# A routed expert layer with a state-space layer: when the first tiles are masked, where the threshold search runs, and how the one-hots lie

## The chip, the cores and the metric

One Trainium2 chip, one of its cores. The metric is the device time of one execution of the kernel in microseconds (us); a lower one is better.

## The reference, cut to what matters

The input is 16 batches of 512 tokens with 256 channels. Each token is normalised; the result goes through a state-space layer (64 states) and through a layer of 8 experts, of which each token uses one.

```python
xn = layernorm(x)
# state-space layer
Bu = einsum('bld,nd->bln', xn, B_w)
h  = causal convolution of Bu with lam ** t          # a first-order recurrence
y  = einsum('bln,dn->bld', h, C_w) + D * xn
# experts
aff   = (xn @ waff.T) / (|xn| * |waff| + 1e-9)       # [16, 512, 8]
cap   = clip(floor(512 * sigmoid(aff.mean() - threshold)), 4, 512)
tcr   = one_hot(argmax(softmax(aff)), 8)
ecr   = rank of the token within its batch and expert < cap
mask  = tcr * ecr
for e in range(8):                                   # masked tokens, exact gelu
    acc += gelu((xn * mask[e]) @ W1[e] + b1[e]) @ W2[e] + b2[e]
out = x + y + acc
```

A token that is not kept by its expert still gets each expert's answer to a zero row, `gelu(b1[e]) @ W2[e] + b2[e]`, so does every token for the experts it does not use.

## The kernel before, in words

The kernel has one function, `moe_ssm_kernel`, with a program for each engine; the programs wait for each other by semaphores, and the order of work on each engine is written out by hand. Line numbers are those of the profile.

**Batches (0 to about 150 us).** A loop over 16 batches normalises, turns, runs the recurrence (VectorE, `tensor_tensor_scan`, L899) and the state products (TensorE, `states_out`, L662). GpSimd adds `D * xn + x` (L381, L385); VectorE adds the state result (`add_y`, L905). Normalised rows and base rows are stored to DRAM. Beside it the expert weights are loaded and split into a high and a low f16 part (ScalarE L513, VectorE `low_part` L928); 12 of 16 weights are ready before the tiles start, four second-layer weights (12 to 15, `LATE`) come later through one buffer, `raw_late`, loaded by SP (L336 to L340).

**Routing.** From the affinities VectorE takes the expert of each token (L1036 to L1046). Two things are then worked out beside each other:

- *The capacity threshold.* VectorE computes the capacity and turns the affinity rows into integer keys (L1052 to L1072). ScalarE finds the key of the last kept token bit by bit: `find` (L563) makes 14 digits on the upper halves, each of three dependent instructions (L565 to L567); VectorE then forms the second keys (`second_digits`, L1127), and `find` makes 16 more digits. `second_half` (L574) is called between digits: after digit 8 it copies the zero rows of the experts out of PSUM (L520), after digit 10 it splits the rows of tile 0 (L586).
- *The slots.* TensorE counts the tokens of each expert (L709, L710). VectorE gives each token a place, a high digit among 78 half tiles and a low digit among 128 rows, and makes one-hots of both in four groups of 16 token columns (`places`, L1110): L1119 and L1124 over 16 x 78 elements, L1123 over 16 x 128. In a group the token column is the outer dimension; the place value is read with stride 0 inside. TensorE multiplies them (`tokens_of`, L729) between the zero rows of the experts (`zero_row`, L713). VectorE turns the product into the token indices of all slots (L1154 to L1161).

**Tiles.** There are 39 tiles of 256 slots (`NT`), each of one expert. GpSimd gathers a tile's normalised rows (`step`, L409: L420), later its base rows (L444), and scatters the result (L434). TensorE turns the rows (`rows_t`, L771), ScalarE and VectorE split them in two f16 parts (L586, L1233), TensorE makes the first product (`up`, L781, 96 matmuls), ScalarE the gelu (L596), VectorE the two parts of h (`h_parts`, L1237), TensorE the second product (`down`, L798, 96 matmuls), and VectorE the result (`result`, L1250: L1255 takes it from PSUM, L1261 applies the mask and adds the base row, L1268 adds the zero rows' sum). On TensorE a step is: rows of tile j+1, up j, down j-1. The first 8 steps (`PEEL`) are written out, the others are a loop of two steps.

**The first two steps** carry what is left of routing. In step 0 VectorE waits for the search's result and makes the kept flags (`kept`, L1167), then the h parts of tile 0. TensorE turns the flags (`kept_rows`, L748), VectorE multiplies the one-hot planes by them (`kept_places`, L1189) and scales the late weights (`late_scales`, L920). In step 1 TensorE multiplies again (`kept_slots`, L761, 64 matmuls), VectorE makes `mask_slot` (`kept_mask`, L1202), and down 0 follows. Only then does SP load the late weights.

Of the kernel before, what the change touches and what calls it, by code (L numbers as in the profile page):

```python
# [11 lines left out]
P = 128  # L12


def moe_ssm_kernel(nc, u, log_lambda, B_w, C_w, D_w, waff, W1, b1, W2, b2, threshold, out, xn_dram, base_dram, num_dram):
# [24 lines left out]
    PEEL = 8  # L40
# [10 lines left out]
    with ExitStack() as ctx:  # L51
# [16 lines left out]
        slot_val = sb("slot_val", B)  # L68
# [60 lines left out]
        lo16 = part(area, (UNITS - 4) * UW, T * P // 2).bitcast(F16).rearrange("p (t l) -> p t l", l=P)  # L129
# [6 lines left out]
        dxn = part(work, 3 * QD, QD)  # L136
        g_bc = part(work, 4 * QD, E * D)
# [5 lines left out]
        planes = [x.bitcast(F16).rearrange("p (t j) -> p t j", j=NS) for x in planes]  # L143
        den = key_hi
# [3 lines left out]
        xnorm, sq0, ratio = pos, hi_f, lo_f  # L148
        hi16, low16 = hi_f.bitcast(F16)[:, 0:T], lo_f.bitcast(F16)[:, 0:T]
# [42 lines left out]
        def psum(name, cols):  # L192
# [7 lines left out]
        ps_bu = [ps_bu0, ps_bu1]  # L200

# [14 lines left out]
            "dve_chain", "r_pool", "bmax_ok", "bmax_out", "bmax_in", "bmax_used", "scales_ok",  # L216
# [6 lines left out]
        def zero_out(i):  # L223

            return [ps_g[:, 0:2 * D], ps_t[:, S:S + 2 * D], ps_y[:, 0:2 * D], ps_y[:, 2 * D:4 * D]][i]
# [36 lines left out]
        def _(sp):  # L262
# [73 lines left out]
            sp.wait_ge(s["mask_ok"], 1)  # L336
# [7 lines left out]
        def _(pool):  # L344
# [16 lines left out]
            link(g.iota(iota_i[:, 0:B], [[S, 4], [1, Q]], base=1, channel_multiplier=Q))  # L361
            link(g.tensor_copy(slot_val[:, :], iota_i[:, 0:B]))
# [46 lines left out]
            def step(m, r, gate_no):  # L409

                t_out, t_base = m - 5, m - 3
                if is_tile(m):
                    wait(pool, s["f_xt"], m - 1)
                    gate(gate_no)
                    g.tensor_copy(idx_x[:, 2 * r:2 * r + 2], idx_all[:, bass.ds(m * 2, 2)]).then_inc(s["ix"], 1)
                    pool.wait_ge(s["ix"], m + 1)
                    gate(gate_no + 1)
                    gate_no = gate_no + 2
                    for h in range(2):
                        g.indirect_dma_start(out=xg[r % 2][:, h * D:(h + 1) * D], out_offset=None, in_=xn_dram,  # L420
                                             in_offset=bass.IndirectOffsetOnAxis(
                                                 ap=idx_x[:, 2 * r + h:2 * r + h + 1], axis=0),
                                             bounds_check=bound, oob_is_err=False).then_inc(gx[r % 2], 16)
                rb = (r + 1) % 4
# [6 lines left out]
                if is_tile(t_out):  # L431
                    ro = (r + 3) % 4
# [15 lines left out]
                return gate_no  # L448
            gates = 0
            for m in range(8):  # L450
                if m == 3:

                    for n in range(8):
                        pool.wait_ge(base_out[n], 16)
                    for p in range(2):
                        g.memset(bg[p], 0.0).then_inc(s["cleared"], 1)
                    pool.wait_ge(s["cleared"], 4)
                gates = step(m, m % 4, gates)
                if m == 2:
                    for e in range(E):  # L460
                        add_zero_row(e)
# [11 lines left out]
        def _(act):  # L473
# [73 lines left out]

            act.wait_ge(s["aff_ok"], 1)
# [782 lines left out]
```

## Time and profile before

| | us |
|---|---|
| median of 3 runs | 661.86 (659.16 to 662.46) |
| the profiled execution | 663.84 |
| its span in the profile | 662.1 |

| engine | busy us | share of the span | instructions |
|---|---|---|---|
| PE (TensorE matmul) | 589.7 | 89% | 4597 |
| PEld (weight load) | 497.0 | 75% | 4598 |
| DVE (VectorE) | 512.2 | 77% | 974 |
| ACT (ScalarE) | 337.3 | 51% | 635 |
| POOL (GpSimd) | 462.6 | 70% | 625 |

The span in 40 slices of 16.6 us, busy tenths:

```profile
PE   2988888858945599999999999999999999999994
DVE  5789989799998979987667768676767676767672
ACT  5776868825799235644433435353535353535340
POOL 1999997920038838888776768787777787788453
PEclk9988868776997799999999999999999999999998
```

A digit is the busy share in tenths, in PEclk the clock that the throttle granted TensorE. Slices 9 to 14 (149 to 248 us) hold routing and the first steps, the others to the right are tile steps alone. A busy PE is not PE at its peak: its ends are modelled. The chain of waits follows the work back from the last instruction; a timeline lists instructions in order of time.

### The profile page before, as it was taken

The page shows a single profiled execution, that of the slowest core. Times are in us where ns is not written, and L with a number is a line of the kernel's source. Part 1 is how long each engine was busy: PE and PEld are TensorE (multiplying, and loading weights), DVE is VectorE, ACT ScalarE, POOL GpSimd, SP SyncE. Part 2 cuts the span into 40 slices and gives each one's busy share as a digit, 9 for nine tenths or more (in the row PEclk, how much of TensorE's full clock was granted, in tenths as well). Part 3 has the DMA queues.
Part 4 walks back from the last instruction along what each step waited for, and adds up shares of the span by engine and source line. Part 5 has one row for each costly group of instructions (what it writes and reads, how often), then busy time and mean ns, then how long its engine had stood idle before and what let it go on. Part 6 is the DMA issues. An engine that isn't in the chain of part 4 may idle for free.

```text
span 662.1 us, 16027 instructions
## 1 busy us (share of the span) xinstructions
PE 589.7 (89%) x4597; PEld 497.0 (75%) x4598; DVE 512.2 (77%) x974; ACT 337.3 (51%) x635; POOL 462.6 (70%) x625
## 2 busy tenths in 40 slices
PE   2988888858945599999999999999999999999994
PEld 1655555546834499898988888989898989898983
DVE  5789989799998979987667768676767676767672
ACT  5776868825799235644433435353535353535340
POOL 1999997920038838888776768787777787788453
PEclk9988868776997799999999999999999999999998
DMA  8985757611801134512212112212112212210100
GB/s 308 413 346 173 253 208 266 230 75 43 274 18 33 40 97 153 169 57 74 72 57 70 54 53 66 75 50 79 49 44 71 67 48 67 63 60 24 51 29 2
DMA packets 33584, 72.58 MB, mean 110 GB/s; under 512 B 6519, under 2 KB 19088, under 8 KB 33552
## 3 DMA queue, kind: packets, MB, share of 16 engines
q1 hardware_dynamic: 21488, 46.67, 19.7%
q0 software_dynamic: 11232, 25.20, 12.4%
q10 hardware_dynamic: 832, 0.31, 0.2%
q8 instruction: 17, 0.28, 0.2%
q14 instruction: 15, 0.12, 0.1%
HBM read 50.64 MB, written 27.00 MB: 117 GB/s over the span
## 4 chain that ended last, share of the span: by engine, by line
PE 69%; DVE 16%; ACT 7%; issue 6%; DMA 1%; POOL 1%; DVEq 0%; SPq 0%; ACTq 0%; POOLq 0%
PE ps_bu L820 10%; PE ps_bu L818 10%; PE ps_bu L819 10%; PE ps_t L793 5%; PE ps_y L795 5%; PE ps_t L794 5%; PE ps_y L794 5%; PE ps_t L795 5%; PE ps_y L793 5%; ACT area L494 2%; PE ps_y L662 2%; PE ps_bu L648 2%; PE ps_t L630 2%; ACT work L565 1%; PE ps_g L777 1%
## 5 line engine op out<-in xcount | busy, mean ns | idle before, releaser
L820 PE MATMUL ps_bu<-area,ring 128*128 x624 | 170.1, 273 | 1.5 <-issue 1.4
L818 PE MATMUL ps_bu<-area,ring 128*128 x624 | 170.1, 273 | 0.3
L819 PE MATMUL ps_bu<-area,ring 128*128 x624 | 170.1, 273 | 0.0
L1247 DVE SCALAR_TENSOR_TENSOR ring<-ring,h_scale 128x512 f16<-128x512 f32 x156 | 117.2, 751 | 5.6
L434 POOL DMA_INDIRECT out<-ring,idx_b x78 | 96.9, 1243 | 19.1 <-issue 14.7
L372 POOL TENSOR_TENSOR small<-ones 128x1 f32<-128x1 f32 x156 | 48.1, 308 | 86.8 <-DVE work L1161 33.4
L420 POOL DMA_INDIRECT work<-xn_rows,idx_x x78 | 87.1, 1117 | 27.1 <-issue 23.9
L444 POOL DMA_INDIRECT work<-base_rows,idx_b x78 | 92.3, 1183 | 18.0 <-issue 15.8
L596 ACT ACTIVATE ring<-ps_t,b1t,inv_in 128x256 f32<-128x256 f32 x156 | 79.2, 560 | 44.7 <-PE ps_t L795 42.4
L596 ACT ACTIVATE ring<-ps_y,b1t,inv_in 128x256 f32<-128x256 f32 x156 | 77.8, 562 | 45.9 <-PE ps_y L795 22.8
L1244 DVE TENSOR_SCALAR ring<-ring,h_scale 128x512 f16<-128x512 f32 x156 | 77.9, 499 | 23.4 <-issue 13.2
L1255 DVE SCALAR_TENSOR_TENSOR ring<-ps_bu,inv_out,work 128x256 f32<-128x256 f32 x78 | 34.1, 479 | 75.3 <-PE ps_bu L820 69.8
L793 PE MATMUL ps_t<-work,area 128*128 128x256 f16 x312 | 86.4, 277 | 0.2 <-issue 0.2
L794 PE MATMUL ps_t<-work,area 128*128 128x256 f16 x312 | 86.3, 277 | 0.0
L795 PE MATMUL ps_t<-work,area 128*128 128x256 f16 x312 | 86.1, 276 | 0.0
L793 PE MATMUL ps_y<-work,area 128*128 128x256 f16 x312 | 85.0, 273 | 0.0
L795 PE MATMUL ps_y<-work,area 128*128 128x256 f16 x312 | 85.0, 273 | 0.0
L794 PE MATMUL ps_y<-work,area 128*128 128x256 f16 x312 | 85.0, 273 | 0.0
L381 POOL TENSOR_TENSOR work<-area,d_bc 128x256 f32<-128x256 f32 x64 | 59.2, 956 | 20.5 <-DMA thr_bc<-L_ffn_affinity_threshold 12.2
L818 PEld LDWEIGHTS ps_bu<-area,ring 128*128 128x128 f16 x624 | 61.0, 98 | 9.1 <-issue 2.1
L820 PEld LDWEIGHTS ps_bu<-area,ring 128*128 128x128 f16 x624 | 61.0, 98 | 8.8 <-issue 1.8
L819 PEld LDWEIGHTS ps_bu<-area,ring 128*128 128x128 f16 x624 | 61.0, 98 | 7.8 <-issue 0.9
(267 smaller groups left out, 1085.0 us busy)
## 6 DMA issues: line engine op xcount, KB each, us to landing
ring<-L_ffn_W SPq DMA_DIRECT2D x14, 1024.0 KB, 6.4
xn_rows<-area SPq DMA_DIRECT2D x8, 1024.0 KB, 9.4
base_rows<-area SPq DMA_DIRECT2D x8, 1024.0 KB, 7.3
area<-L_attn_u SPq DMA_DIRECT2D x7, 1024.0 KB, 18.2
work<-L_ffn_W SPq DMA_DIRECT2D x5, 1024.0 KB, 9.0
work<-xn_rows,idx_x POOLq DMA_INDIRECT x78
work<-base_rows,idx_b POOLq DMA_INDIRECT x78
out<-ring,idx_b POOLq DMA_INDIRECT x78
```

Of the source, the lines that this page charges most:

```text
L420: g.indirect_dma_start(out=xg[r % 2][:, h * D:(h + 1) * D], out_offset=None, in_=xn_dram, in_offset=bass.IndirectOffsetOnAxis(ap=idx_x[:, ...
L434: g.indirect_dma_start(out=out_rows, out_offset=bass.IndirectOffsetOnAxis(ap=idx_b[:, 2 * ro + h:2 * ro + h + 1], axis=0), in_=og[ro % 2][ ...
L444: g.indirect_dma_start(out=bg[rb % 2][:, h * D:(h + 1) * D], out_offset=None, in_=base_dram, in_offset=bass.IndirectOffsetOnAxis(ap=idx_b[ ...
L596: ins = a.activation(h32[:, c * W:(c + 1) * W], ps_h[qt][:, c % CQ * W:(c % CQ + 1) * W], ACT.Gelu, bias=b1t[:, bass.ds(e * C + c, 1)], sc ...
L793: t.matmul(dst, wh, xhi[p][:, k, :], start=(k == 0), stop=False)
L794: t.matmul(dst, wh, xlo[p][:, k, :], start=False, stop=False)
L795: last = t.matmul(dst, wl, xhi[p][:, k, :], start=False, stop=(k == K - 1))
L818: t.matmul(dst, hh, wh, start=(c == 0), stop=False)
L819: t.matmul(dst, hh, wl, start=False, stop=False)
L820: last = t.matmul(dst, hl, wh, start=False, stop=(c == C - 1))
L1244: v.tensor_scalar(hhi[p][:, cs], h32[:, cs], h_scale[:, bass.ds(e, 1)], None, ALU.mult).then_inc(s["f_hhi"], 1)
L1247: v.scalar_tensor_tensor(out=hlo[p][:, cs], in0=h32[:, cs], scalar=h_scale[:, bass.ds(e, 1)], in1=hhi[p][:, cs], op0=ALU.mult, op1=ALU.sub ...
```

## The change

1. **First tiles drained unmasked.** `result` is split into `drained` (from PSUM) and `result` (mask, base row, sum). `kept`, `kept_rows`, `kept_places`, `kept_slots` and `kept_mask` move from steps 0 and 1 to steps 2 to 4; the results of tiles 0 and 1 are masked in VectorE's fourth step, those of 2 to 4 after it. GpSimd issues the row gathers of tiles 5 to 7 ahead of the first scatters. SP waits for `slots_ok` in place of `mask_ok` before the late weights, and these are split in steps 4 to 7. `PEEL` is 10.
2. **The search.** The first keys are made before the experts' one-hot and its scan; the second keys are made by GpSimd. The exp and gelu tables are loaded by two dummy activations. The zero rows are copied after digit 4 (the last one after digit 5), tile 0 is split after digit 5. The zero rows lie in other PSUM banks. TensorE's order after the last batch becomes: affinities turned, their sum, state product 14, zero rows 0 and 1, counts, state product 15, zero rows 2 and 3, then token products 0 to 3 each followed by one of the zero rows 4 to 7. The low parts 10 and 11 move behind the first split of VectorE, the maxima of weights 12 and 13 ahead of it.
3. **One-hots.** The token column is the innermost dimension of the one-hots; `iota16` is repeated for it by GpSimd into `irep`; `slot_val` and the kept values are f16. TensorE's operands then have a stride of 16 elements.

The diff, cut to its core:

```diff
@@ layouts @@
-        lo16 = part(area, (UNITS - 4) * UW, T * P // 2).bitcast(F16).rearrange("p (t l) -> p t l", l=P)
+        lo16 = [part(area, (UNITS - 4) * UW + n * TG * P // 2, TG * P // 2).bitcast(F16).rearrange("p (l t) -> p l t", t=TG)
+                for n in range(4)]
+        irep = part(work, 3 * QD, TG * P // 2).bitcast(F16).rearrange("p (l t) -> p l t", t=TG)
-        planes = [x.bitcast(F16).rearrange("p (t j) -> p t j", j=NS) for x in planes]
+        planes = [x.bitcast(F16).rearrange("p (j t) -> p j t", t=TG) for x in planes]
@@ sync @@
-            sp.wait_ge(s["mask_ok"], 1)
+            sp.wait_ge(s["slots_ok"], 1)
@@ gpsimd @@
+            pool.wait_ge(s["dx_ok"], 2 * B)
+            g.tensor_copy(irep, iota16[:, :].rearrange("p (l a) -> p l a", a=1).to_broadcast([P, P, TG])).then_inc(s["irep_ok"], 1)
+            pool.wait_ge(s["low_ok"], 1)
+            pool.wait_ge(s["hi_found"], 1)
+            g.tensor_scalar(search[:, 4:5], search[:, 0:1], -1.0, None, ALU.mult)
+            link(g.tensor_scalar(key_hi, key_hi, search[:, 0:1], 2.0 ** 17, ALU.add, ALU.mult))
+            g.memset(search[:, 0:1], -(2.0 ** 15 - 0.5))
+            g.tensor_tensor(key_hi, key_hi, low_half, ALU.add).then_inc(s["key_lo_ok"], 1)
...
+            for m in range(5, 8):
+                gates = rows_in(m, m % 4, gates)
+            for m in range(5, 8):
+                gates = out_and_base(m - 5, m - 3, (m + 3) % 4, (m + 1) % 4, gates)
@@ scalar @@
             def zero_rows(i):
-                if i == 0:
-                    act.wait_ge(s["g_pe"], E)
-                    act.wait_ge(s["wsum_ok"], EARLY + 1)
+                act.wait_ge(s["g_pe"], E if i == 3 else E - 1)
+                act.wait_ge(s["wsum_ok"], EARLY + 1)
...
+            a.activation(small[:, 62:63], lam_c, ACT.Exp)
             act.wait_ge(s["aff_ok"], 1)
...
+            a.activation(small[:, 62:63], lam_c, ACT.Gelu)
...
             def second_half(n):
-                if n == 8:
-                    for i in range(E // 2):
+                if n == 4:
+                    for i in range(3):
                         zero_rows(i)
-                if n == 10:
+                if n == 5:
                     split_x(0, 0)
+                    zero_rows(3)
...
-                split_x(j + 1, 1 - p)
-                hidden(j)
+                if isinstance(j, int) and j in (3, 4):
+                    hidden(j)
+                    split_x(j + 1, 1 - p)
+                else:
+                    split_x(j + 1, 1 - p)
+                    hidden(j)
@@ tensor @@
...
+            zero_row(0)
+            zero_row(1)
             pe.wait_ge(s["oh_ok"], 1)
...
             states_out(B - 1)
...
+            zero_row(2)
+            zero_row(3)
             tokens_of(0)
...
+                if first not in (3, 4):
+                    rows_t(j + 1, 1 - p, k + p)
...
                 up(j, p)
...
+                if first == 3:
                     kept_rows()
...
+                if first == 4:
+                    pe.wait_ge(s["mask_ok"], 1)
+                    rows_t(5, 1, 2)
+                if first > 0:
+                    down(j - 1, 1 - p)
+                if first == 3:
+                    pe.wait_ge(s["kept_read"], 1)
+                    rows_t(4, 0, 2)
                     kept_slots()
@@ vector @@
-                link(v.tensor_tensor(planes[g], same(NS), of(hi16, NS), ALU.is_equal))
+                link(v.tensor_tensor(planes[g], irep[:, 0:NS, :], of(hi16[:, cols], NS), ALU.is_equal))
...
-                v.tensor_tensor(lo16[:, g * TG:(g + 1) * TG, :], same(P), of(low16, P), ALU.is_equal)
+                v.tensor_tensor(lo16[g], irep, of(low16[:, cols], P), ALU.is_equal)
...
-            largest(14)
-            low_part(10, raw[2])
-            low_part(11, raw[3])
+            for n in (14, 12, 13):
+                largest(n)
...
             tile_scales()
             x_low(0, 0)
+            largest(15)
+            low_part(10, raw[2])
+            low_part(11, raw[3])
+            x_low(1, 1)
+            h_parts(0, 0)
+            late_scales()
+            x_low(2, 0)
+            h_parts(1, 1)
+            out_scales()
+            drained(0, 0)
+            x_low(3, 1)
+            kept()
+            h_parts(2, 0)
+            drained(1, 1)
+            kept_places()
+            x_low(4, 0)
+            h_parts(3, 1)
+            kept_mask()
+            dve.wait_ge(s["mask_ok"], 1)
+            dve.wait_ge(s["c_ok"], E)
+            result(0, 0, 0)
+            result(1, 1, 0)
+            drained(2, 0)
+            x_low(5, 1)
+            h_parts(4, 0)
+            low_part(EARLY, raw_late)
+            result(2, 0, 1)
+            drained(3, 1)
...
```

## Rows read from the trace of the kernel before

**Rows 1.** The chain that ended last, in order of time: start us, us, what
```profile
230.45 4.22 PE ps_bu L765 x64
...
294.49 0.44 PE ps_num L777 x4
...
305.41 0.44 PE ps_g L777 x4
```

**Rows 2.** ScalarE's timeline: start us, us, engine line op, tiles [idle before <-releaser]
```profile
150.86 1.28 ACT L553 ACT_TABLE_LOAD   x1
...
157.95 0.72 ACT L565 ACTIVATE work<-work,small 128x512 f16<-128x512 f32 x1 [5.53 <-DVE work L1072]
...
182.44 0.72 ACT L565 ACTIVATE work<-work,small 128x512 f16<-128x512 f32 x1 [3.52 <-DVE work L1132]
...
210.18 1.28 ACT L596 ACT_TABLE_LOAD   x1 [0.30 <-PE ps_y L795]
```

**Rows 3.** VectorE's timeline, the same columns
```profile
152.96 0.68 DVE L1052 TENSOR_SCALAR_CACHE_REDUCE work<-work 128x512 f32<-128x512 f32 x1
...
161.39 0.69 DVE L1093 TENSOR_TENSOR work<-work,small 128x512 f32<-128x512 f32 x1
...
171.01 1.45 DVE L1119 TENSOR_TENSOR area<-iota,work 128x1248 f16<-128x1248 f16 x1
...
172.49 2.29 DVE L1123 TENSOR_TENSOR area<-iota,work 128x2048 f16<-128x2048 f16 x1
...
174.70 1.45 DVE L1124 TENSOR_TENSOR area<-area,slot_val 128x1248 f16<-128x1248 f16 x1
...
191.31 0.20 DVE L1161 CAST work<-work 128x78 int32<-128x78 f32 x1
...
210.52 0.14 DVE L1172 CAST bits<-small 128x1 int32<-128x1 f32 x1
...
216.80 0.48 DVE L1244 TENSOR_SCALAR ring<-ring,h_scale 128x512 f16<-128x512 f32 x1 [0.35 <-issue]
```

**Rows 4.** TensorE's timeline, the same columns
```profile
145.38 3.80 PE L662 MATMUL ps_y<-ct,work 64*128 64x256 f32 x8
...
156.89 8.34 PE L724 MATMUL ps_g<-ring,gelu_b 128*128 128x256 f32 x32
...
165.06 7.07 PE L724 MATMUL ps_t<-ring,gelu_b 128*128 128x256 f32 x32
...
187.53 0.76 PE L733 MATMUL ps_num<-work,area 128*128 128x78 f16 x16 [1.96 <-DVE work L1124]
...
188.13 3.69 PE L724 MATMUL ps_y<-area,gelu_b 128*128 128x256 f32 x16
...
199.15 1.09 PE L777 MATMUL ps_num<-ident,work 128*128 128x128 f32 x4 [7.33 <-DMA work<-xn_rows,idx_x]
...
203.69 1.12 PE L777 MATMUL ps_g<-ident,work 128*128 128x128 f32 x4 [3.45 <-DMA work<-xn_rows,idx_x]
...
216.50 0.75 PE L752 MATMUL ps_bu<-ident,work 128*128 128x128 f32 x4 [4.33 <-DVE work L1187]
...
234.50 0.27 PE L818 MATMUL ps_bu<-area,ring 128*128 x1
```

**Rows 5.** The stretch 217 to 221: length, busy time of each engine, granted clock, DMA
```profile
217.00:221.00 4.00, 4.00 (x24) 3.06 (x23) 3.86 (x8) 0.94 (x2) 3.46 (x5) 0.57 0.14 43
```

**Rows 6.** GpSimd's timeline, columns as in rows 2
```profile
129.01 7.40 POOL L385 TENSOR_TENSOR area<-area,work 128x256 f32<-128x256 f32 x4
...
194.41 2.78 POOL L420 DMA_INDIRECT work<-xn_rows,idx_x  x1 [0.31 <-issue]
...
202.78 1.04 POOL L420 DMA_INDIRECT work<-xn_rows,idx_x  x1 [0.40 <-issue]
```

**Rows 7.** TensorE's weight loads, grouped by line and form: count, busy us, mean ns
```profile
L662 PEld LDWEIGHTS ps_y<-ct,work 64*128 64x128 f32 x128 | 33.7, 325 | 14.0 <-issue 11.4
...
L671 PEld LDWEIGHTS ps_g<-ring,ones 128*128 128x128 f32 x4 | 0.5, 190 | 0.1
```

More of the change, by code:

```diff
@@ L407, in is_tile, with rows_in, out_and_base @@
                 return not isinstance(j, int) or 0 <= j < NT
[L409 to L424, printed above, removed]
+            def rows_in(m, r, gate_no):
+                wait(pool, s["f_xt"], m - 1)
+                gate(gate_no)
+                g.tensor_copy(idx_x[:, 2 * r:2 * r + 2], idx_all[:, bass.ds(m * 2, 2)]).then_inc(s["ix"], 1)
+                pool.wait_ge(s["ix"], m + 1)
+                gate(gate_no + 1)
+                for h in range(2):
+                    g.indirect_dma_start(out=xg[r % 2][:, h * D:(h + 1) * D], out_offset=None, in_=xn_dram,
+                                         in_offset=bass.IndirectOffsetOnAxis(
+                                             ap=idx_x[:, 2 * r + h:2 * r + h + 1], axis=0),
+                                         bounds_check=bound, oob_is_err=False).then_inc(gx[r % 2], 16)
+                return gate_no + 2
+            def out_and_base(t_out, t_base, ro, rb, gate_no):
                 if is_tile(t_out):
@@ L1002, in denominators @@
                 link(v.reciprocal(rden, den))
+            order, first = small[:, 40:48], small[:, 81:85]
             for b in range(B):
@@ L1015, in _ @@
                     link(v.memset(cnt[:, 0:1], 0.0))
+                    v.tensor_scalar(order, iota_f[:, 0:E], -1.0, float(E), ALU.mult, ALU.add)
+                    link(v.tensor_scalar(first, iota_f[:, 0:4], float(TOKENS // 4), None, ALU.mult))
                     square_norms()
@@ L1037, in _ @@
             link(v.tensor_tensor(te(gap), te(aff), bt_(rowmax), ALU.subtract))
[L1038 to L1039 removed]
+            link(v.scalar_tensor_tensor(out=te(pick), in0=te(gap), scalar=NEAR, in1=be_(order),
                                         op0=ALU.is_ge, op1=ALU.mult))
             link(v.tensor_reduce(best, te(pick), AX.X, ALU.max))
[L1042 to L1047 removed]
             dve.wait_ge(s["rows_ok"], 1)
@@ L1072, in _ @@
             v.tensor_copy(key_hi, key_i).then_inc(s["key_hi_ok"], 1)
+            link(v.tensor_tensor(et(oh), be_(order), bt_(best), ALU.is_equal))
+            link(v.tensor_tensor_scan(scan_e, ones[:, 0:1].to_broadcast([P, TE]), oh, 0.0, ALU.mult, ALU.add))
+            so_far = scan_e.rearrange("p (e t) -> p e t", e=E)[:, :, T - 1]
+            v.tensor_copy(rc16[:], so_far).then_inc(s["oh_ok"], 1)
+            add_y(B - 2)
             dve.wait_ge(s["key_hi_ok"], 1)
             link(v.tensor_scalar(key_i, eq_rows.bitcast(I32), 0xFFFF, None, ALU.bitwise_and))
-            link(v.tensor_copy(eq_rows, key_i))
-            low_half = eq_rows
+            v.tensor_copy(low_half, key_i).then_inc(s["low_ok"], 1)
             dve.wait_ge(s["counts_ok"], 1)
@@ L1272, in step @@
             def step(j, p, k):
[L1273 to L1274 removed]
                 x_low(j + 1, 1 - p)
[L1276 to L1277 removed]
                 h_parts(j, p)
[L1279 to L1289 removed]
+                if isinstance(j, int) and j < 4 + LATE:
+                    low_part(EARLY + j - 4, raw_late)
+                drained(j - 1, 1 - p)
+                result(j - 1, 1 - p, k - 1 + p)
             tile_scales()
             x_low(0, 0)
[L1292 to L1294 removed]
+            largest(15)
[26 more added lines that the diff above has]
+            drained(3, 1)
+            x_low(6, 0)
+            h_parts(5, 1)
+            low_part(EARLY + 1, raw_late)
+            result(3, 1, 1)
+            drained(4, 0)
+            result(4, 0, 2)
+            for j in range(6, PEEL):
                 step(j, j % 2, j // 2)
```

167 lines of the change are left out of this document (66 added, 101 removed).

## The prediction

> **What bounds the kernel now.** I read the chain of waits first. From about 235 us it is TensorE, nearly without a break: tile steps 10.92 us apart (294.49, 305.41) [rows 1]. 39 tiles make 426 us; nothing in the change shortens them. What can move is when the first down product starts, 234.50, right after the 64 kept-slot matmuls that start at 230.45 [rows 1], and what is put between steps later.
>
> Before that the chain is ScalarE's search: 14 digits from 157.95 (1.5 each), a hole of 3.52 until VectorE has made the second keys, 16 digits from 182.44, with four copies of zero rows and the first split inside, 0.5 to 0.6 each. Then come the second split, a table load of 1.28 at 210.18, and the first gelu at 211.48 [rows 2]. VectorE turns the search's result into kept flags from 210.52 (5.9) before the first h parts at 216.80, then makes kept places (four multiplies of 1.4, the shape of the one-hots) and late scales (1.6) [rows 3]. TensorE idles 4.33 ahead of the kept transposes and again before 230.45; in 217 to 221 it is granted 0.57 on average, that is mostly 1.2 GHz where the later steps have 2.4 [rows 4, 5].
>
> Beside the search runs the slot chain: routing counts, one-hots on VectorE, token products on TensorE between the zero rows, the slot indices at 191.51, gathers by GpSimd, and TensorE's transposes of tile 0 at 199.15 and tile 1 at 203.69 [rows 3, 4]. It has slack now. The question is which chain ends last afterwards.
>
> **The change, part by part,** on the profiled execution's clock (663.84 us, 1.98 above the median of 661.86; I carry the difference over to the median).
>
> 1. Start of the search. The one-hot of the expert, its scan, the copy and one add leave the way to the first keys; an exp table load is issued ahead of its wait, a gelu load after it, so neither stays in the way. The load stands before the affinity sum, so I let the row copy end at 150.6 (150.86 now). From 152.96 to 157.92 the threshold steps take 4.96 [rows 2, 3]: started at 150.65, the search begins at 155.6 and its first half ends at 176.6.
>
> 2. Second keys on GpSimd. Two passes over 512 elements. Four of 256 cost it 7.40 beside a busy VectorE [rows 6]: at worst 3.7 a pass of 512, 7.4; at best what VectorE needed, 1.2. I take 3.5 (VectorE is busy only in part of it): keys at 180.1, digits 0 to 4 done at 187.6. Behind it on GpSimd stand the clearing of the row buffers and every gather; they wait for the indices anyway.
>
> 3. One-hots. A group of three takes 5.06 (starts 171.01, 172.49, 174.70, the last with 1.37 to the next) [rows 3]. With all operands 16-bit and innermost unit stride, the bounds are nothing and half the time per element. For half: a one-input pass over 512 takes 0.48, a two-input one 0.69 [rows 3], so the engine has a faster way; no two-input row shows it. I take half: 2.7 a group. The Trainium skill (VectorE: DVE Perf Modes, "The perf-mode tier table") has two-input 16-bit operations at two elements a cycle; by it the group takes 2.6, and the sum stays.
>
> 4. TensorE's queue now decides the indices. In order: one state product (3.8 at half clock) from 150.35, zero rows 0 and 1 (8.2, partly at half clock), counts, at 162.5; state product 2.1; zero rows 2 and 3 (7.1) to 171.7, by the same work now [rows 4]. VectorE needs after the counts some eleven small steps of 0.2, then 4.56 as now from 161.39 to the first group (165.95): it starts groups at 169.3 and ends them at 172.0, 174.7, 177.4 and 180.1. The products then go at TensorE's pace, 0.6 each (187.53 to 188.13) with zero rows of 3.65 between [rows 4]: the fourth ends at 185.5. Six short steps as now (2.5) give the indices at 188.1, 3.4 earlier. One-hots of up to 4.2 a group would do as well.
>
> 5. Gathers. The first one's second half took 2.78 beside two-input low parts on VectorE; the third's took 1.04 and 1.00 beside one-input maxima [rows 6]. The low parts now come after the maxima. So tile 0's transposes start 5.6 after the indices (7.64 now), at 193.7, tile 1's 9.0 after (12.18 now), at 197.1 [rows 4]. With no such gain both are 2 to 3 later; kept for the range.
>
> 6. Waits inside the search. After digit 4 ScalarE now waits for all zero rows but the last and for the maximum of weight 14, behind the indices: 188.1+0.3+2.2 = 190.6, a stall of 3. Three copies and digit 5: 193.7. The split of tile 0 waits for its transposes (end 194.8): 195.4, last copy 195.9. Ten digits of 1.5: 210.9. Split, and the first gelu at 211.5 with no table load. So the gelu is where it was: the start gained in 1 and 2 is spent waiting. Queued behind the two waits is the whole rest of the search, and behind that the gelu.
>
> 7. First tiles. Up product 0 runs at 198.2 to 204.5, before the gelu as now. Up product 1 starts at 212.5 and costs 5.24+1.5 (half clock after idling, as now) to 219.3. h parts run at 212.6 to 217.4 with nothing in front. Down product 0 starts at 219.3: **15.2 earlier** than 234.5.
>
> 8. What comes back. In steps 3 and 4 TensorE does the kept transposes (0.6) and kept slots: 64 at 0.042, the pace of the token products, 2.7 (4.05 now, after idling) [rows 1, 4]. **+3.3.** On VectorE: x low, kept flags 5.9 (226.9 to 232.9), h parts 2 to 237.7, drain of tile 1, kept places 241.3 to 246.0 (multiplies at 0.72; at 1.37 to 248.6). TensorE comes to them after down 2, transposes 4, at 247.0: no stall, 1.0 of cover. x low 4 at 248.3, h parts 3 to 253.1, mask 253.4; TensorE asks for the mask at 255.0. Behind that wait stand transposes 5 and down 3, covered by 1.6.
>
> 9. Catching up. Results 0 to 4 and low parts 12 to 15 crowd VectorE, steps 4 to 7. The late weights now leave SP after the kept places (246.0); each chain of landing, high part and low part takes about one step, as now, and I reckon 0 to 3 of cover before each down product. The held-back out and base gathers cost GpSimd 5.4 a pair after result 0 (254.9); base rows of tile 2 land at 266.2, a stall of 1.0 on VectorE that TensorE doesn't see. Taken as nothing; up to 3 kept for the range.
>
> 10. At no cost: the token column copy on GpSimd (2048 elements; idle there 136.4 to 157.1), constants moved into the loop, two more unrolled steps, drain and result split in two (same instructions).
>
> Sum: -15.2+3.3 = **-11.9**: 663.84 becomes 651.9, the median 661.86 becomes 650.0.
>
> **Rivals.**
>
> A. The one-hots stay at 5.06. Groups end at 189.5, indices at 192.7, all of 6 and 7 is 4.6 later; kept places 2.6 later cost TensorE 1.6. -5.7: 656.2. For: no two-input operation in the trace runs faster. Against: until now one operand had stride 0 innermost.
>
> B. Strided reads cost a little. The token and kept matmuls now step 32 bytes between elements, weights and moving side. Strided f32 weights (64 rows) took 325 ns on average against 190 unstrided, over unlike clocks [rows 7]. Against: the four kept transposes, strided too, took 0.75, between the 0.44 of unstrided ones in a later step and their 1.09 after idling [rows 1, 4]. With 0.05 on each of 128 matmuls, half ahead of the indices: +6.4, 656.4.
>
> C. Slower: the same place, a large price. If each of the 128 costs 0.135 more, the whole difference of [rows 7], 17.3 is lost, 8.6 before the indices and 8.6 in step 3: 667.3. It is slower than before from 0.093 each, and by over 0.5% from 0.12. No row shows a strided 16-bit operand. The Trainium skill (SBUF — State Buffer, "Door 1: The DMA port swizzle") speaks against the change here: 16-byte lines, with a penalty when each access opens a new one, that is every element of these. It gives no size.
>
> D. Gathers don't get faster and catching up stalls: +2 and +2 to 3, 654.5.
>
> E. The stall of 6 is absent, the indices coming earlier than I reckon (full clock sooner on TensorE): the search would end near 180.1+24+2.6 = 206.7 (copies and split 2.6), the gelu 4 earlier: 646.
>
> **How the numbers follow.** Sum as reckoned 0.48; A 0.12; B 0.13; C 0.04; D 0.15; E 0.08. The range reaches over E's, D's, A's and B's values: 645 to 659. A measurement of this kernel can tell about 0.5%, 3.3 us, from no change. Above 658.5 lie C (0.04, slower) and the dear ends of A, B and D (stalls added to them), 0.08: faster 0.88, same 0.08, slower 0.04.
>
> **What would show it.** Right: one-hot groups near 2.7; indices near 188; two holes in ScalarE's search, after digits 4 and 5, none before its last ten digits; no table load at the first gelu; first down product near 219 and kept-slot matmuls near 247, 0.042 apart, TensorE unbroken after 212. Wrong: strided matmuls over 0.09 apart (B, C); one-hots at 5.06 (A); a gelu at 207 (E); holes on TensorE in steps 3 to 7 at the mask, the kept read or a late weight (D).

## The result and the profile after

The changed kernel takes **675.71 us** (median of 4 runs, 675.16 to 677.28), the kernel before beside it 661.42: a ratio of 1.0225, 95% interval 1.0192 to 1.0257. It is slower by 2.25%; the prediction had 650.0 and 645 to 659.

| profiled execution | before | after |
|---|---|---|
| span | 662.1 | 675.5 |
| TensorE busy | 589.7 | 604.9 |
| VectorE busy | 512.2 | 499.9 |
| slot indices done | 191.5 | 200.5 |
| first gelu | 211.5 | 224.2 |
| first down product | 234.5 | 232.8 |
| up product of tile 5 / tile 8 | 272.9 / 305.7 | 283.3 / 322.9 |

VectorE saves 12 us and TensorE, which does the same 4597 matmuls, is busy for 15 more. In TensorE's timeline after, first the products of a token group, then the kept-slot products and the first matmul of the up product of tile 4 behind them, last a pause of 2.42 ahead of the up product of tile 6, for which VectorE is late:

```profile
176.19 2.59 PE L758 MATMUL ps_num<-area 128*128 128x78 f16 x16 [0.42 <-DVE area L1166]
...
260.34 7.30 PE L797 MATMUL ps_g<-area 128*128 128x78 f16 x48
267.46 2.55 PE L797 MATMUL ps_g<-work,area 128*128 128x78 f16 x16
269.83 0.39 PE L825 MATMUL ps_t<-work,area 128*128 128x256 f16 x1
...
296.76 0.28 PE L825 MATMUL ps_t<-work,area 128*128 128x256 f16 x1 [2.42 <-DVE work L1261]
```

16 token products took 0.76 before [rows 4]; they take 2.4 to 2.6 now, 0.15 each, and so do the 64 kept-slot products (9.67 in all). Behind the latter the up product of tile 4 takes 7.48 where others take 5.40. The windows of that stretch (busy time and count of TensorE, its weight loads, VectorE, ScalarE and GpSimd), with the granted clock third from the end (0.69: for most of it 1.2 GHz, after a stretch of strided products without a pause; e12, strided too, has 0.65 there, and e2 below, without the large step, 1.00 and an up product of 5.40):

```profile
240.00:260.00 20.00, 20.00 (x185) 17.99 (x183) 15.22 (x30) 8.15 (x16) 1.73 (x2) 1.00 0.06 15
260.00:270.00 10.00, 10.00 (x70) 9.81 (x69) 5.37 (x9) 0.60 (x1) 2.77 (x5) 0.69 0.41 131
270.00:280.00 10.00, 10.00 (x76) 8.16 (x74) 5.05 (x11) 5.61 (x10) 1.54 (x4) 0.80 0.01 2
```

The fifth busy column is GpSimd's: 1.73 us in 20. That row comes back below.

Where the loss arises can be read from the start of the up products on TensorE. At tile 2 the kernel after is 1.7 us ahead of the kernel before; by tile 5 it is 10.4 behind (the kept-slot products and the slow up product of tile 4 lie between them); by tile 8 it is 17.2 behind. From there to the end it wins 3.9 back, because the kernel before has 4.4 us of late pauses in its trace and this one 0.5. So the difference of the spans is 13.4 (14.3 in the medians). Nothing in the change aimed at those 3.9, and no run explains them.

ScalarE's timeline after, to be held beside [rows 2]: the first digit on the second keys, the first copy of zero rows, the split of tile 0, the first gelu. Then VectorE's, beside [rows 3]: a one-hot, the wait ahead of the indices, the indices:

```profile
183.81 0.72 ACT L592 ACTIVATE work<-work,small 128x512 f16<-128x512 f32 x1 [4.71 <-POOL work L403]
...
202.82 0.58 ACT L544 COPY work<-ps_t 128x512 f32<-128x512 f32 x1 [11.53 <-DVE wsum L980]
...
207.55 0.60 ACT L615 ACTIVATE work<-ps_num 128x512 f16<-128x512 f32 x1 [1.81 <-PE ps_num L809]
...
224.22 1.93 ACT L625 ACTIVATE ring<-ps_t,b1t,inv_in 128x256 f32<-128x256 f32 x4 [0.24 <-issue]
```

```profile
174.19 1.23 DVE L1165 TENSOR_TENSOR area<-work 128x2048 f16<-128x2048 f16 x1
...
198.05 0.48 DVE L1184 SCALAR_TENSOR_TENSOR work<-ps_num,small 128x312 f32<-128x312 f32 x1 [11.13 <-PE ps_num L758]
...
200.31 0.20 DVE L1191 CAST work<-work 128x78 int32<-128x78 f32 x1
```

So VectorE's one-hots are fast as hoped and it then stands 11.13 for the products. After digit 4 the search now waits for the maximum of weight 14, which VectorE makes behind the indices: it stands 11.53.

### The profile page after: what moved, and what is told of

It reads as the page before. It is cut to its first block, busy times and chain, and to the rows that moved or that the text cites. A ratio compares the mean times of both kernels' runs of the same rounds, so it can differ in the third digit from the quotient of the medians.

```text
span 675.5 us, 15993 instructions
## 1 busy us (share of the span) xinstructions
PE 604.9 (90%) x4597; PEld 510.8 (76%) x4598; DVE 499.9 (74%) x970; ACT 339.3 (50%) x637; POOL 459.5 (68%) x630
## 4 chain that ended last, share of the span: by engine, by line
PE 70%; DVE 11%; issue 7%; ACT 6%; DMA 3%; POOL 3%; DVEq 0%; ACTq 0%; SPq 0%; POOLq 0%
PE ps_bu L849 9%; PE ps_bu L851 9%; PE ps_bu L850 9%; PE ps_t L825 5%; PE ps_t L826 5%; PE ps_t L827 5%; PE ps_y L825 5%; PE ps_y L827 5%; PE ps_y L826 5%; PE ps_y L695 2%; PE ps_t L663 2%; ACT area L519 2%; PE ps_bu L681 2%; PE ps_bu L748 2%; PE ps_num L758 1%
## 5 line engine op out<-in xcount | busy, mean ns | idle before, releaser
L448 POOL DMA_INDIRECT out<-ring,idx_b x78 | 92.6, 1187 | 18.3 <-issue 13.4
L458 POOL DMA_INDIRECT work<-base_rows,idx_b x78 | 91.5, 1173 | 18.0 <-issue 15.2
L433 POOL DMA_INDIRECT work<-xn_rows,idx_x x78 | 83.1, 1066 | 28.2 <-issue 23.7
L825 PE MATMUL ps_t<-work,area 128*128 128x256 f16 x312 | 88.1, 282 | 10.2 <-ACT ring L625 7.0
L625 ACT ACTIVATE ring<-ps_y,b1t,inv_in 128x256 f32<-128x256 f32 x156 | 79.4, 560 | 22.4 <-PE ps_y L827 22.4
L826 PE MATMUL ps_t<-work,area 128*128 128x256 f16 x312 | 88.1, 282 | 0.0
L827 PE MATMUL ps_t<-work,area 128*128 128x256 f16 x312 | 87.9, 282 | 0.0
L387 POOL TENSOR_TENSOR work<-area,d_bc 128x256 f32<-128x256 f32 x64 | 61.3, 989 | 22.5 <-DMA thr_bc<-L_ffn_affinity_threshold 12.2
```

What stands on the lines that cost most here:

```text
L448: g.indirect_dma_start(out=out_rows, out_offset=bass.IndirectOffsetOnAxis(ap=idx_b[:, 2 * ro + h:2 * ro + h + 1], axis=0), in_=og[ro % 2][ ...
L458: g.indirect_dma_start(out=bg[rb % 2][:, h * D:(h + 1) * D], out_offset=None, in_=base_dram, in_offset=bass.IndirectOffsetOnAxis(ap=idx_b[ ...
L625: ins = a.activation(h32[:, c * W:(c + 1) * W], ps_h[qt][:, c % CQ * W:(c % CQ + 1) * W], ACT.Gelu, bias=b1t[:, bass.ds(e * C + c, 1)], sc ...
L825: t.matmul(dst, wh, xhi[p][:, k, :], start=(k == 0), stop=False)
L826: t.matmul(dst, wh, xlo[p][:, k, :], start=False, stop=False)
L827: last = t.matmul(dst, wl, xhi[p][:, k, :], start=False, stop=(k == K - 1))
```

## The experiments

All times are medians of the runs of a kernel. The ratio is to the kernel before, run beside it on the same chip (median 663.7 for e1 to e4, 663.5 for e5 to e8, 664.4 for e9 to e12, 662.6 for e13 and e14). Kernels of different groups are compared by their ratios. The diffs are cut to the lines that matter.

### Which operand pays

**e1**: both one-hots with the token outermost again, all else as changed.

```diff
-planes = [x.bitcast(F16).rearrange("p (j t) -> p j t", t=TG) for x in planes]
+planes = [x.bitcast(F16).rearrange("p (t j) -> p t j", t=TG) for x in planes]
-lo16[g][:, :, i], planes[g][:, :, i],
+lo16[g][:, i, :], planes[g][:, i, :],
```

> The changed kernel with the one-hots laid out as before (token column outermost, TensorE's operands contiguous); all else as changed. Theory S, strided operands: each of the 128 one-hot matmuls goes back from 0.15 to 0.04 and the steps after them run at full clock again; one-hot groups go back from 2.7 to 5.06 on VectorE, which then sets the indices (near 197 for 200.5). The kept slots take 2.7 for 9.7. Time about 661 to 664, no difference from before. Rival O, the order: the copies of zero rows and the first split wait inside the search for the indices, and this is what makes the kernel slower: 672 or more, since they still wait.

Measured: 675.56, ratio 1.0193 (1.0159 to 1.0226). A miss for theory S: the products are back at 0.76 a group, but a one-hot takes 2.29 and a group 5.06 again, so the search stands 7.11 for the second keys and 7.22 ahead of the copies. Theory O had the time, and the second of these waits; the first it did not name. ScalarE's timeline:

```profile
184.84 0.72 ACT L592 ACTIVATE work<-work,small 128x512 f16<-128x512 f32 x1 [7.11 <-POOL work L403]
...
199.53 0.59 ACT L544 COPY work<-ps_t 128x512 f32<-128x512 f32 x1 [7.22 <-DVE wsum L980]
```

The new order costs 12 us with the old layout, so it isn't free either.

**e2**: two token columns innermost. A matmul operand then steps 4 bytes, while VectorE still has two neighbours of unit stride.

```diff
-lo16 = [... .rearrange("p (l t) -> p l t", t=TG)
+lo16 = [... .rearrange("p (o l t) -> p o l t", l=P, t=2)
-lo16[g][:, :, i], planes[g][:, :, i],
+lo16[g][:, i // 2, :, i % 2], planes[g][:, i // 2, :, i % 2],
```

> The changed kernel with two token columns innermost in place of sixteen: VectorE still has unit stride in pairs, TensorE's operands step 4 bytes in place of 32. Theory S with a price by distance (a new line at every element): matmuls at 0.04, groups at 2.7 to 3, indices near 191, time about 654 to 658. If any stride costs as much as this one: matmuls at 0.15 and 675. Rival O: 672 or more.

Measured: 664.58, ratio 1.0018 (1.0001 to 1.0035): of the 2.25% lost, 2.07 are gone, 13.7 us. The pace is theory S's, the time lies between S (654 to 658) and O (672 or more): something else costs too. One-hots stay at 1.23, and TensorE's timeline shows unstrided pace for both kinds of product:

```profile
174.40 0.78 PE L759 MATMUL ps_num<-area 128*128 128x78 f16 x16 [0.42 <-DVE area L1170]
...
249.30 1.98 PE L798 MATMUL ps_g<-area 128*128 128x78 f16 x48
```

**e3** and **e4**: 16 columns innermost for one operand alone, pairs for the other: the weights (low one-hot) in e3, the moving planes in e4.

> As the run with pairs, but the stationary operand (the low one-hot) keeps its 32 byte step and only the moving operand (the planes) has pairs. If the stationary side carries the price: matmuls 0.15 apart and about 674; if the moving side does: 0.04 apart and about 656; if both share it: between.

> The other way round: the planes (moving, 78 columns) step 32 bytes, the low one-hot (stationary, 128 columns) has pairs. If the moving side carries the price: 0.15 apart and about 674; if the stationary side does: 0.04 apart and about 656.

Measured, one run each: 670.31, between the forecasts, and 682.48, above the 674 expected. The first group of each, e3 then e4, in TensorE's timeline:

```profile
177.59 1.20 PE L759 MATMUL ps_num<-area 128*128 128x78 f16 x16 [0.90 <-DVE area L1170]
```

```profile
178.28 2.45 PE L759 MATMUL ps_num<-area 128*128 128x78 f16 x16 [1.19 <-DVE area L1170]
```

The moving side carries nearly the full price, 0.14 a product (0.15 in the kernel after) against 0.04; strided weights alone cost about 0.02 more each.

### What e2 leaves open

e2 starts its first down product at 221.8, 12.7 ahead of before, and has 1.7 left at tile 8. In its timelines GpSimd stands still, and then VectorE does, for base rows:

```profile
249.56 0.19 POOL L379 TENSOR_TENSOR small<-ones 128x1 f32<-128x1 f32 x1 [18.54 <-PE ps_num L810]
```

The windows of 240 to 260, before and in e2, show what this leaves undone: GpSimd (fifth busy column) is busy for 16.58 before, where its stand ends at 240.4 after 9.32, and for 4.68 in e2.

```profile
240.00:260.00 20.00, 20.00 (x186) 17.97 (x184) 18.41 (x30) 13.12 (x20) 16.58 (x23) 1.00 0.40 130
```

```profile
240.00:260.00 20.00, 19.96 (x225) 18.16 (x223) 14.59 (x26) 9.81 (x19) 4.68 (x9) 1.00 0.22 68
```

VectorE in e2:

```profile
274.40 0.88 DVE L1296 SCALAR_TENSOR_TENSOR ring<-ring,work 128x256 f32<-128x256 f32 x2 [6.34 <-DMA work<-base_rows,idx_b]
```

The table is read from TensorE's timelines: start of the up products of tiles 2, 5 and 8, what steps 5 to 7 took over 3 x 10.92, and what the 29 steps from there to tile 37 took over 10.92 each, called late pauses below. There is one trace of each kernel, and the late pauses are those of that one execution: e6's trace is of a run of 665.37, where its median is 662.80, and e9's of one of 660.98, where its median is 664.56.

| kernel | tile 2 | tile 5 | tile 8 | over, 5 to 8 | over, 8 to 37 |
|---|---|---|---|---|---|
| before | 240.2 | 272.9 | 305.7 | 0.0 | 4.4 |
| after | 238.5 | 283.3 | 322.9 | 6.9 | 0.5 |
| e1 old layout | 235.9 | 275.1 | 315.7 | 7.8 | 4.4 |
| e2 pairs | 227.4 | 263.3 | 304.0 | 7.9 | 5.6 |
| e5 order on GpSimd | 228.5 | 264.4 | 304.4 | 7.3 | 9.1 |
| e6 search | 222.7 | 258.5 | 299.0 | 7.8 | 12.5 |
| e7 both | 221.9 | 257.8 | 299.0 | 8.4 | 9.3 |
| e8 before, pairs | 234.6 | 267.3 | 300.1 | 0.0 | 4.9 |
| e9 without stores | 227.5 | 263.4 | 298.4 | 2.3 | 8.7 |
| e10 8 written out | 221.7 | 257.5 | 298.4 | 8.1 | 11.9 |
| e11 down first | 231.3 | 264.0 | 298.3 | 1.5 | 8.1 |
| e12 eights | 237.5 | 282.3 | 322.3 | 7.2 | 14.0 |
| e13 before, owed | 234.2 | 271.1 | 307.2 | 3.4 | 0.5 |
| e14 down first, table | 231.9 | 264.6 | 298.6 | 1.2 | 0.7 |

### What eats the front's gain

**e5** (on e2): the result of tile 0 and the base rows of tile 2 are issued ahead of the rows of tile 7.

```diff
-            for m in range(5, 8):
+            for m in range(5, 7):
                 gates = rows_in(m, m % 4, gates)
+            gates = out_and_base(0, 2, 0, 2, gates)
+            gates = rows_in(7, 3, gates)
```

> The changed kernel with its columns in pairs (as e2), and on GpSimd the results of tile 0 and the base rows of tile 2 are issued ahead of the rows of tile 7. Theory K (what the deferred tiles owe is paid in steps 4 to 8: VectorE is busy there for 10.4 us of each 10.92 us tile and GpSimd for 9 to 12, and VectorE stood 6.34 us for the base rows of tile 2): the base rows are issued about 4 us earlier, VectorE waits 1 to 3 us in place of 6.34, the pause of TensorE ahead of the up product of tile 6 falls from 3.4 to under 1 us, and the time from 664.6 to about 662 (660.5 to 663.5). Rival F (what is missing was lost ahead of the first gelu, in the search's waits, and the later pauses only stand in the shadow of something else): 664.6 within 1.

Measured: 670.86, ratio 1.0119 (1.0082 to 1.0155). A miss for both theories. The wait moved instead of going: the pause ahead of tile 6 fell to 0.6 and one came ahead of tile 7, whose rows are now the late ones (TensorE's timeline below). VectorE waits for base rows twice, 4.54 and 5.52, in place of once 6.34. Tile 8 is where it was in e2. The ratio is 1.0% above e2's all the same, some 6.7 us; the profiled run, the fastest of six, shows 3.5 of that in late pauses, the rest is unexplained.

```profile
290.69 0.94 PE L812 MATMUL ps_num<-ident,work 128*128 128x128 f32 x4 [3.54 <-DMA work<-xn_rows,idx_x]
```

**e6** (on e2): copies and split moved to digits where their input is ready.

```diff
-                if n == 4:
+                if n == 6:
...
-                if n == 5:
+                if n == 8:
```

> The changed kernel in pairs, with the copies of the zero rows after digit 6 in place of 4 and the split of tile 0 after digit 8 in place of 5, where both find their input ready: the 2.96 and 1.82 us in which ScalarE stood in the second half of the search go. First gelu and first down product about 4.5 us earlier by both theories. Theory K: steps 4 to 8 give it back, since GpSimd and VectorE set their ends there; the up product of tile 8 comes less than 1.5 us earlier and the time is 663 to 665. Rival F: all of it arrives, 660 (659 to 661).

Measured: 662.80, ratio 0.9993 (0.9974 to 1.0011). Tile 2 starts 4.8 earlier, as expected by both, and so does tile 8 (299.0 against theory K's 302.5 or more), but the median gains only 1.8. In the traces late pauses grow from 5.6 to 12.5, though e6's is of one of its slower runs. K was right on the time to 0.2 and wrong on the place; neither theory as put fits.

**e7**: both edits.

> Both edits of e5 and e6 together. Theory K: about as e5, 660.5 to 663, since the front's gain meets the same bound. If instead both edits add: 657.5 to 659.

Measured: 663.58, ratio 0.9988 (0.9960 to 1.0017). They don't add.

**e8**: the kernel before, one-hots in pairs with the f16 values and the repeated `iota16` that they take, nothing else.

```diff
-planes = [x.bitcast(F16).rearrange("p (t j) -> p t j", j=NS) for x in planes]
+planes = [x.bitcast(F16).rearrange("p (o j t) -> p o j t", j=NS, t=2) for x in planes]
```

> The kernel before with nothing but the one-hots in pairs of token columns. One-hot groups fall from 5.06 to about 2.7 us and the four multiplies of the kept places from 1.45 to about 0.8 each. The second keys wait for the search alone (stall 3.52 to about 1.5), the kept places end 2.6 us earlier, so the first down product starts some 4 us earlier (234.5 to 230.5), and nothing is deferred. Theory K: what is won in front is kept, since every tile from the second on is finished in its own step; 657.5 (655.5 to 660). Rival F' (whatever is won in front is given back before tile 10 in any order): 661 within 1.

Measured: **657.14, ratio 0.9906 (0.9877 to 0.9935)**, with tile 8 5.6 earlier and no step between 2 and 8 over 10.92. K's 657.5 is met; F' falls. The layout by itself is worth 6.4 us. The new order, e2 against e8, costs 7.4 net: e2 is 7.2 ahead of e8 at tile 2, 4.0 ahead at tile 5 and 3.9 behind at tile 8.

### Whose debt

**e9** (on e2): the indirect stores of the results of tiles 0 to 3, and the waits for them, are left out; these rows are missing in its output.

```diff
-                if is_tile(t_out):
+                if is_tile(t_out) and not (isinstance(t_out, int) and t_out < 4):
                     for h in range(2):
                         g.indirect_dma_start(out=out_rows,
```

> The changed kernel in pairs (e2, 664.58) without the eight indirect stores of the results of tiles 0 to 3: their rows are left out of the output, every other operation stays. Theory G (the bound behind the deferred tiles is GpSimd: in e2 it stands still for 18.5 us ahead of 249.6, then has work without a pause for over 100 us, at 16.5 busy us in each 20, against 15.5 in its steady pace; every index copy and gather of the later tiles is late by this debt): about 10.5 us of its debt of 18.5 go, the up products of tiles 6 to 8 come 3 to 6 us earlier, and the waits of tiles 10 to 17 shrink to what the kernel before has; 658 (656 to 661). Rival V (VectorE alone carries the debt, with four results of 1.6 us each and the late low parts): 664.5 within 1.5.

Measured: the trace as theory G has it, tile 8 5.5 earlier and VectorE's wait for the base rows down from 6.34 to 0.84:

```profile
269.00 0.88 DVE L1296 SCALAR_TENSOR_TENSOR ring<-ring,work 128x256 f32<-128x256 f32 x2 [0.84 <-DMA work<-base_rows,idx_b]
```

V would have left that wait. But the time is 664.56 over a wide 659.03 to 671.91, ratio 0.9981 (0.9943 to 1.0020), and late pauses did not shrink (8.7). That half of G is a miss.

**e10** (on e6): `PEEL = 8`.

> Kernel e6 (662.80) with 8 tiles written out in place of 10, as in the kernel before. Rival H (the pauses of tiles 9 to 17 are ScalarE and the others fetching code, more of it since two more tiles are written out): 659 to 660. Theory G: the pauses are there because nothing has slack while GpSimd is in debt, so the number of tiles written out does not matter: 662.8 within 1.2.

Measured: 664.12, ratio 0.9987 (0.9957 to 1.0017), late pauses 11.9. e6's ratio, 0.9993, lies inside the interval: two more tiles written out make no difference, and H falls as put.

**e11** (on e8): down product of tile 0 ahead of the kept-slot products.

```diff
-                if isinstance(j, int) and j == 1:
-                    kept_slots()
                 if not (isinstance(j, int) and j == 0):
                     down(j - 1, 1 - p)
+                if isinstance(j, int) and j == 1:
+                    kept_slots()
```

> Kernel e8 (657.14, the kernel before in pairs) with the down product of tile 0 ahead of the kept-slot products in TensorE's queue; nothing is deferred on VectorE or GpSimd. By e8's rows the up product of tile 1 ends at 222.0 and the results h of tile 0 are ready at 218.7, so the down product runs 222 to 227.4 where TensorE stood 3.0 us for the kept places, and the kept-slot products run 227.4 to 231.3: the up product of tile 2 starts at 231.5 in place of 234.57. If the gain stays, as theory G says where GpSimd owes nothing: 654 (652.5 to 656). If the mask comes too late for the result of tile 0: 657 within 1.

Measured: 658.38 (654.52 to 662.30), ratio 0.9883 (0.9833 to 0.9933). Tile 2 starts at 231.3 as expected (3.3 earlier), but at tile 8 1.8 of it are left, and the time is above the 652.5 to 656 expected. e8's ratio lies inside the interval, so the times don't tell the two apart.

**e12**: 8 columns innermost, a step of 16 bytes.

> The changed kernel with 8 token columns innermost in both one-hots (a step of 16 bytes between the elements of an operand in place of 32 in the change and 4 in the pairs). Theory S (the price of a strided moving operand is paid once its elements stand 16 bytes or more apart): token products at 0.14 us each as in the change, 675. Rival P (the price grows with the step): half of it, 0.09 us each, 669 to 671. If no price below 32 bytes: 0.038 each, 664.6.

Measured, one run: 690.22. A group takes 2.5, as with 32 bytes, so the price is whole at 16 bytes and absent at 4. The time is far over all three forecasts: its tile 8 is where the kernel after has it, and 14 us are late pauses (the table's last column).

```profile
175.17 2.53 PE L759 MATMUL ps_num<-area 128*128 128x78 f16 x16 [0.42 <-DVE area L1170]
```

### The debt alone

**e13** (on e8): on GpSimd alone, rows of tiles 5 to 7 ahead of results 0 to 2 and base rows 2 to 4.

```diff
-                gates = step(m, m % 4, gates)
+                gates = step(m, m % 4, gates, rest=m < 5)
...
+            for m in range(5, 8):
+                gates = step(m, m % 4, gates, rows=False)
```

> Kernel e8 (the kernel before in pairs, 657.14, ratio 0.9906) with one part of the change alone: on GpSimd the rows of tiles 5 to 7 are asked for ahead of the results of tiles 0 to 2 and the base rows of tiles 2 to 4. All else is in the old order. Theory G: the base rows of tile 2 are asked for only after tile 5 is transposed, VectorE stands for them, TensorE loses 3 to 8 us by tile 8 and little of it comes back: 662 (660 to 666), ratio 0.995 to 1.004. Rival V (the deferred work of VectorE is the cause, GpSimd's order is not): 657 to 658, ratio 0.989 to 0.992.

Measured: 664.32, ratio 1.0029 (1.0007 to 1.0050), 1.2% above e8's, 8 us. Windows of 240 to 260, e8 then e13, GpSimd's busy time in the fifth column, then VectorE's timeline of e13:

```profile
240.00:260.00 20.00, 20.00 (x185) 18.02 (x184) 18.96 (x28) 11.76 (x18) 17.19 (x21) 1.00 0.49 150
```

```profile
240.00:260.00 20.00, 20.00 (x186) 18.01 (x184) 15.29 (x21) 11.82 (x18) 5.38 (x12) 1.00 0.35 111
```

```profile
267.00 0.88 DVE L1271 SCALAR_TENSOR_TENSOR ring<-ring,work 128x256 f32<-128x256 f32 x2 [10.20 <-DMA work<-base_rows,idx_b]
```

GpSimd leaves 12 us of work undone there and does not make it up soon: it is busy for 17.2 of the next 20 us where e8 is for 17.1. VectorE waits 10.20, and tile 8 is 7.2 later than in e8. Not all of that is waiting: TensorE, idle for part of 265 to 270 (busy 2.82 of 5), is granted 0.50 of full speed from 270 to 275 (1.2 GHz), by an estimate from these windows some 3 of the 7.2. In e2's pauses the granted clock stayed at 1.00. V gave 657 to 658 and falls; G's 662 (660 to 666) holds.

**e14** (on e11): the gelu's table is loaded behind the exp.

```diff
+            a.activation(small[:, 86:87], lam_c, ACT.Gelu)
```

> Kernel e11 (kernel before in pairs, down product of tile 0 ahead of the kept-slot products) with the gelu's table loaded right behind the exp. The 1.28 us load leaves ScalarE's path, but the up product of tile 1 waits for the kept tokens' transposes at 213.7 in e8, not for the gelu (over at 212.9), so by the trace of e8 the load was covered: as e11, ratio 0.986 to 0.989, that is 654 to 656 where the kernel before takes 663.5. If the load did count: 1.3 less.

Measured: **651.77 (650.68 to 653.11), ratio 0.9836 (0.9804 to 0.9869)**, the best of all. The ratio is below the 0.986 to 0.989 expected, near the 1.3 us less that were put for a load that counts; but its interval overlaps e11's (0.9833 to 0.9933), so only the gain over e8 is clear. TensorE's timeline in front is that of e11 to 0.6; as in e11 the kept-slot products follow the down product without a pause (3.00 in e8):

```profile
229.00 1.98 PE L772 MATMUL ps_bu<-area 128*128 128x78 f16 x48
```

What differs from e11 is the last column, 0.7 against 8.1, which no edit here aimed at.

**What stays open: the late pauses.** They go with waits of ScalarE at its splits and gelus that the profile puts down to "remote", that is to no instruction or transfer that it can name. Summed over ScalarE's timeline from 300 us these are 10.3 before, 11.7 in e2, 21.6 in e6, 8.0 in e8, 11.9 in e11 and 3.7 in e14, and 0.0 after and 1.0 in e13, whose late pauses are 0.5: nearly the order of the table's last column (before and e8 change places). One from e6:

```profile
313.77 0.60 ACT L616 ACTIVATE work<-ps_num 128x512 f16<-128x512 f32 x1 [7.66 <-remote]
```

They hit kernels of both orders, and neither the debt (e9) nor the code written out (e10) set them. Nor does the loading of instructions explain the later ones: from 345 to 640 us e6's profile has no packet in an instruction queue, while ScalarE has such waits at 369.37 (2.14), 536.80 (2.01) and 603.63 (1.97). No run isolates their cause, and the part of e14's gain over e8 beyond the 3 us of e11's edit may be theirs.

## Why the prediction was wrong

By its own steps:

1. *Start of the search*: 158.1 for 155.6. The batch loop ended 3 us later (its last routing at 147.9, at 144.8 before); in the other kernels with the changed front its last routing lay between 145.5 and 149.5, with the old front between 144.2 and 146.5, so part of it is the run's.
2. *Second keys on GpSimd*: a wait of 4.71 where 3.5 was taken, inside the bounds; 3.8 to 7.1 in the experiments.
3. *One-hots*: right, 1.23 for the big one and 2.69 a group.
4. *TensorE's queue*: **the step that failed first.** It took 0.6 a group of products; a group took 2.4 to 2.6. Four groups cost 7 more ahead of the indices, the zero rows behind the first group 1.6 (5.29 for 3.65), and the counts came 3.8 late with the loop and the clock: 200.5 for 188.1. The mechanism had been seen as rivals B and C, at 0.05 and 0.135 for each product; measured was 0.11. C, with the sign that came out, had a chance of 0.04, because the one row on strided weights was of another type, over unlike clocks, and I let it fall to B. C reckoned 17.3 for the strides; at 0.11 each its sum gives 14, and the ratios of after and of e2 differ by 13.7 us. The Trainium skill's rule (SBUF — State Buffer, "Door 1: The DMA port swizzle") of 16-byte lines that each want two accesses agrees with e2 (a step of 4 bytes, no price) and e12 (16 bytes, whole price). The same note lets 16-bit elements be stepped over by 8 for free; the measurement says otherwise, as e12 steps by 8 and pays in full. The rule spoke against the change, and weighed too little.
5. *Gathers*: tile 0's transposes came 5.9 after the indices, where 5.6 was taken.
6. *Waits inside the search*: the place was right (after digits 4 and 5), the size 11.53 for 3, all of it step 4's delay. With pairs it is 2.96.
7. *First tiles*: down product 0 at 232.8 for 219.3. In e2, without the strides' price, it is at 221.8, 2.5 late: its search starts only 0.5 late (156.1), but VectorE reads the counts at 164.8 where 162.5 was taken, the indices come at 190.2, 2.1 late, and the copies, the split and the gelu (213.9 for 211.5) follow them.
8. *What comes back*: 9.67 for 2.7, and 2.1 more on the up product behind it at half clock; in e2 2.58, as reckoned.
9. *Catching up*: **the second step that failed.** It was "taken as nothing; up to 3". It costs 6.9 in the trace after and, without the large strides, 7.9 in e2's, where e8's steps 5 to 7 lose nothing; without the stores of four tiles (e9) 2.3 of it are left. The sum looked at who waits for a mask or a weight, and priced what GpSimd had to issue, but only as far as the base rows of tile 2, with a cover of some microseconds. It did not ask what GpSimd would owe. Before, it is busy in 16.6 to 17.0 of each 20 us from 240 to 320, so what is held back finds little room; e13 shows a loss of this size with that one edit (tile 8 7.2 later, in part by the clock; 8 us in the time).
10. *No cost*: holds as far as seen; the two unrolled steps are e10.

By the ratios the layout in pairs gives 0.94% (e8), the new order on top of it takes 1.12% (e2 against e8) and the strides 2.07% (after against e2): -6, +7.4 and +13.7 us. By the trace: where -15.2 was forecast, -1.7 was left (step 4); the 3.3 that come back were 12.1 (tiles 2 to 5, steps 4 and 8); steps 5 to 7, taken as nothing, cost 6.9 (step 9). That is 17.2, and the 3.9 of fewer late pauses, which nobody forecast, bring it to 13.4: in that the kernel was lucky. Of rival D, catching up was right in kind, with under half the size. E's missing stall is e6, which gained 1.8 and not 4.

The likeliest case had 0.48 and faster 0.88 in all, because the two unseen prices, both flagged, were each let stand at their kind end.

## What to carry to other kernels

Before an operation that a busy engine issues is put off, add up that engine's busy share in the steps after: with 17 of 20 us taken, a wait is a debt. Here 12 us of work put off in e13 cost 7 at tile 8 and 8 in the time, about as much as the whole new order gains in front (7.2 at tile 2, e2 against e8). When a layout is turned round for one engine, check the step it gives the others: two elements innermost gave VectorE all its gain (1.23 against 2.29) and TensorE's moving side a step of 4 bytes for nothing, where 8 or 16 innermost took nearly four times as long per product. Four innermost (8 bytes) was not run. And a front's gain is only worth what arrives some tiles later: read the same product's start in both traces at several tiles, not at the first one.

## What the runs showed of the hardware

- A product with a 16-bit moving operand of 78 columns took about 0.04 us at a step of 2 or 4 bytes (e1, e2) and 0.14 to 0.15 at 16 or 32 (e12, e4, after); with weights at 32 bytes and the moving side at 4 about 0.062 (e3).
- Around 64 products at the large step without a pause the granted clock was 0.69 in a window of 10 us (0.65 in e12), and the next up product took 7.48 for 5.40; with pairs (e2) it was 1.00 and 5.40.
- Two neighbours of unit stride in the innermost place were enough for VectorE's fast rate on f16 pairs: 2048 elements in 1.23, as with 16, against 2.29 with one operand's innermost stride 0.
- Two f32 passes over 512 elements on GpSimd kept the search waiting 3.8 to 7.1 us, where VectorE's kept it 1.34 once it was free (e8).
